# Transposes on TensorE written as float32 products of 32 columns with the identity

## The reference

```python
x = x + _L0_attn_ref(_layernorm(x), Wq, bq, Wk, bk, Wv, bv, Wo, bo, relative_k, relative_v)
x = x + _L0_ffn_ref(_layernorm(x), router_w, router_b, w1, b1, w2, b2, sw1, sb1, sw2, sb2)
...
scores = jnp.einsum('bhld,bhrd->bhlr', Q, K) * scale
scores = scores + jnp.einsum('bhld,lrd->bhlr', Q, rel_k)
attn = jax.nn.softmax(scores, axis=-1)
out = jnp.einsum('bhlr,bhrd->bhld', attn, V)
out = out + jnp.einsum('bhlr,lrd->bhld', attn, rel_v)
```

## Time and profile before

| | us |
|---|---|
| median of 3 runs | 2068.07 (2067.51 to 2069.0) |
| profiled execution, its own time | 2070.57 |
| profiled execution, span of the trace | 2068.8 |
| TensorE busy | 2037.4 |
| DVE busy | 1605.3 |
| ACT busy | 1507.0 |
| GpSimd busy | 1212.4 |

### The profile page before, as it was taken

The page is one execution under the profiler, slowest core; times in us unless marked ns, Lnnn a source line. Parts: engine busy times, 40 slices in busy tenths (PEclk is TensorE's granted clock), DMA queues, the critical chain, the costliest instruction groups (busy, mean ns, idle before and its releaser), DMA issues.

```text
span 2068.8 us, 86886 instructions
## 1 busy us (share of the span) xinstructions
PE 2037.4 (98%) x37378; PEld 1512.6 (73%) x37378; DVE 1605.3 (78%) x3788; ACT 1507.0 (73%) x3333; POOL 1212.4 (59%) x1283
## 2 busy tenths in 40 slices
PE   5999999999999999999999999999999999999999
PEld 3777777777777777777777777777777777777777
DVE  5877897788778877877897788778886767676765
ACT  3767676777677776667667666666666888888887
POOL 4554464456445544554455446444443898989888
PEclk8999999999999999999999999999999999999999
DMA  4212211221221122112211321223122221222120
GB/s 112 74 54 67 76 48 55 76 65 53 56 80 55 49 66 73 56 46 69 76 53 46 84 67 46 57 73 67 46 54 50 27 31 23 33 27 32 24 30 12
DMA packets 256658, 113.05 MB, mean 55 GB/s; under 512 B 143018, under 2 KB 253492, under 8 KB 256276
## 3 DMA queue, kind: packets, MB, share of 16 engines
q1 hardware_dynamic: 255796, 107.10, 21.3%
q10 hardware_dynamic: 480, 0.39, 0.1%
HBM read 83.34 MB, written 8.39 MB: 44 GB/s over the span
## 4 chain that ended last, share of the span: by engine, by line
PE 91%; DVE 4%; ACT 2%; POOL 1%; issue 1%; DMA 1%; SPq 0%; ACTq 0%; DVEq 0%; POOLq 0%
PE ps L1548 21%; PE ps L1483 12%; PE ps L1568 10%; PE ps L1490 8%; PE ps L1578 8%; PE ps L1501 7%; PE ps L1765 3%; PE ps L1767 3%; PE ps L1766 3%; PE ps L1747 3%; PE ps L1749 3%; PE ps L1748 3%; PE ps L1586 1%; ACT probs L777 1%; PE ps L1464 1%; DVE keys L1235 1%
## 5 line engine op out<-in xcount | busy, mean ns | idle before, releaser
L777 ACT ACTIVATE probs<-ps,neg_max 128x512 f32<-128x512 f32 x1024 | 690.4, 686 | 338.7 <-DVE neg_max L1003 338.6
L1003 DVE TENSOR_REDUCE neg_max<-ps 128x1 f32<-128x512 f32 x1024 | 635.8, 683 | 148.9 <-PE ps L1490 144.8
L549 POOL TENSOR_TENSOR stat_hi<-q_twice,mask8h 128x1024 f16<-128x1024 f16 x128 | 242.6, 1895 | 533.4 <-PE ps L1490 481.7
L1548 PE MATMUL ps<-const,probs 128*128 128x128 f32 x4096 | 497.3, 274 | 1.3 <-ACT probs L777 0.5
L1548 PEld LDWEIGHTS ps<-const,probs 128*128 128x128 f32 x4096 | 454.0, 141 | 29.5 <-issue 15.8
L1008 DVE COPY probs_t<-ps 128x512 f32<-128x512 f32 x512 | 339.9, 684 | 89.8 <-PE ps L1548 87.3
L767 ACT ACTIVATE probs_t<-ps 128x512 f32<-128x512 f32 x512 | 278.8, 595 | 131.8 <-PE ps L1548 129.5
L679 POOL TENSOR_TENSOR probs_t<-probs,probs_t 128x1024 f16<-128x1024 f32 x160 | 341.3, 2156 | 31.1 <-ACT probs_t L859 30.4
L1483 PE MATMUL ps<-keys,stat_hi 128*32 128x512 f16 x4096 | 317.4, 383 | 0.0
L1490 PE MATMUL ps<-rk_split,stat_rel 96*32 96x512 f16 (+2 forms) x4096 | 281.4, 340 | 0.0
L565 POOL TENSOR_TENSOR stat_rel<-q_rel,mask4h 96x1024 f16<-96x1024 f16 x128 | 250.6, 1958 | 49.7 <-PE ps L1490 30.6
(11 more groups left out here) (173 smaller groups left out, 2864.6 us busy)
## 6 DMA issues: line engine op xcount, KB each, us to landing
rv_step<-in_rv_win SPq DMA_DIRECT2D x128, 512.0 KB, 3.9
keys<-keys SPq DMA_DIRECT2D x56, 96.0 KB, 2.7
x_pair<-in_x SPq DMA_DIRECT2D x8, 512.0 KB, 4.4
rel_scratch<-rel_t SPq DMA_DIRECT2D x256, 16.0 KB, 3.2
x_pair<-in_x SPq DMA_DIRECT2D x16, 256.0 KB, 3.1
x_pair<-rel_scratch SPq DMA_DIRECT2D x64, 64.0 KB, 4.3
out<-keys SPq DMA_DIRECT2D x16, 256.0 KB, 2.3
q_twice<-q_hi SPq DMA_DIRECT2D x28, 128.0 KB, 3.0
```

The lines of the kernel that those rows point to most:

```text
L777: nc.scalar.activation(probs[:, q, :], ps[:, i, :], ACT.Exp, bias=neg_max[:, q:q + 1], accum_out=row_sum[parity][:, s * QUADS + q:s * QUAD ...
L1003: nc.vector.tensor_reduce(neg_max[:, q:q + 1], ps[:, i, :], op=ALU.max, axis=AX_X, negate=True).then_inc(max_done, 1)
L1548: last = nc.tensor.transpose(ps[:, bank, rt * P:(rt + 1) * P], probs[:, q, rt * P:(rt + 1) * P], ident)
```

## The change

Four places no longer use the transposing form: the probabilities (transposes), the relative sums (rel_transposes), the rows (rows_t) and the natural queries (natural_queries). A new helper, transposed, takes the data in slices of 32 columns as the stationary operand and multiplies each with the identity in a plain float32 matmul; each lands in its 32 partitions of the same PSUM bank. The tile rel_o loses its unused half, and its memset on GpSimd is gone with it. The FFN part's own transposes (relative_sums, prepare_h, prepare_comb) and the float16 ones of relative_queries stay.

```diff
-        rel_o = sb("rel_o", [P, 4, 32])
+        rel_o = sb("rel_o", [P, 2, 32])
...
-        SETUP_POOL = 11
+        SETUP_POOL = 10
...
-            nc.gpsimd.memset(rel_o[:], 0.0).then_inc(setup_pool, 1)
...
+            def transposed(out, rows):
+                for g in range(rows.shape[1] // 32):
+                    last = nc.tensor.matmul(out[32 * g:32 * g + 32, :], rows[:, 32 * g:32 * g + 32], ident, start=True, stop=True, skip_group_check=True)
+                return last
...
-                    last = nc.tensor.transpose(ps[:, bank, t * P:(t + 1) * P], x_pair[:, half * 4 + t, :], ident)
+                    last = transposed(ps[:, bank, t * P:(t + 1) * P], x_pair[:, half * 4 + t, :])
...
-                    last = nc.tensor.transpose(ps[:, bank, l * D:(l + 1) * D], rows, ident)
+                    last = transposed(ps[:, bank, l * D:(l + 1) * D], rows)
...
-                        last = nc.tensor.transpose(ps[:, bank, rt * P:(rt + 1) * P], probs[:, q, rt * P:(rt + 1) * P], ident)
+                        last = transposed(ps[:, bank, rt * P:(rt + 1) * P], probs[:, q, rt * P:(rt + 1) * P])
...
-                nc.tensor.transpose(ps[:, AV_BANK, 3 * P:4 * P], rel_o[:].rearrange("p a r -> p (a r)"), ident).then_inc(rel_tr, 1)
+                transposed(ps[0:64, AV_BANK, 3 * P:4 * P], rel_o[:].rearrange("p a r -> p (a r)")).then_inc(rel_tr, 1)
```

More of the change, by code:

```diff
@@ L1031, in reduce_relative @@
                 dve.wait_ge(rel_tr, START + pair * STEPS + s)
-                nc.vector.tensor_reduce(rel_o[:, 0:2, :].rearrange("p a (g h) -> p (a g) h", h=DK), r_masked[:].rearrange("p g l h -> p g h l"),
+                nc.vector.tensor_reduce(rel_o[:].rearrange("p a (g h) -> p (a g) h", h=DK), r_masked[:].rearrange("p g l h -> p g h l"),
                                         op=ALU.add, axis=AX_X).then_inc(rel_reduced, 1)
```

## The result

The changed kernel takes 2527.49 us (median of 4 runs, 2526.15 to 2529.51), the kernel before 2067.9 in the same series. The ratio is 1.222, with a 95% interval of 1.220 to 1.224. The forecast was 2522. The two profiled executions differ by 455.6 us (2526.15 and 2070.57), the medians by 459.6.

The account below looks back on a forecast made before the run. TensorE, busy 98% of the span, was taken as the bound. The terms 448 + 14 + 11 + 2 - 27 + 11 - 5 gave +454 us, a median of 2522; range 2500 to 2538, upper end 2560 with a slightly late supply.

Parts of the forecast that it names:

- The count of matmuls: On TensorE, a plain float32 product is carried out as two matmuls, each with its own weight load, a transpose as one.
- Term 1: Probabilities: 256 calls of 16 squares, each set of four narrow products 0.219 us against 0.109 for a transpose: +448 us.
- term 5: Weight loads of the probabilities' transposes that stood idle 11.5 us for exponentials: waits end inside longer calls, -5 us.
- Term 2: Relative sums at L1586: 128 squares, two narrow products each, 0.22 us for 0.11: +14 us, at the least no added time.
- Term 3: Rows and natural queries made ahead, 14 calls each, 112 squares: +11 us together, and +2 for 16 squares at the start.
- Term 4: Switches of tile shape between narrow products and full width: -27 us for those lost, +11 us for new ones.
- the 178 and 77 places: Rounds that lose a switch into the transposes (178, 0.15 us each) or gain one behind a full-width piece (77, 0.14 each).
- The first rival: An identity product costs no more than a transpose, one matmul, 0.109 us for a set: some 2052 to 2056, chance 0.04.
- The factor of four: Transposing mode is four times faster for float32, so +1423 us less 21 for switches and waits: about 3470, chance 0.02.
- The range: The forecast's own range for the time, 2500 to 2538 us, from the bounds of terms 2, 4, 5 and the set price.
- The second rival: Instructions don't arrive fast enough for TensorE: at 23 ns each a round takes 10.3 us, about 3420 in all; chance 0.08.

Follow-up runs that it names:

- the first experiment: The changed kernel with one plain float32 product of full width for each square in place of four of 32 columns: 2610.3 us, ratio 1.262.

## Why the prediction was right

- **The count of matmuls** (two for a plain float32 product) held: 32768 entries, and at full width, where nothing but the form changed, 8192 for 4096 and the same loss. The prediction's "nothing but the transposing form has one" is true of float32 alone: half-precision products such as L1483 have one entry each (4096 in the trace, 4096 in the program).
- **Term 1, the price of a set** (+448). A call takes 3.49 us, 0.218 for each set. The run with the probabilities back gives 450 for this term, the waits of term 5 and the late rounds below together; 448 - 5 + some 8 would make 451.
- **Term 2, the sums** (+14). The upper bound was the right one: 0.21 in the chain, and 25 of the expected 27 us with their switches.
- **Term 3, rows and natural queries** (+13 with the start). 12.7 by the difference of two runs.
- **Term 4, switches** (-27 + 11). In the changed kernel 0.14 us into narrow tiles stands in the chain, as forecast, and the 0.15 behind L1583 is gone (3.49 and not 3.65). Measured by itself with a tiny matmul a switch was 0.10. No run varied the 178 and 77 places alone, but the two traces can be laid side by side, each round from its first L1501 (L1506) to the next one. The median round got longer by 1.60 us without a piece and 1.70 with sums (forecast 1.60 and 1.71), by 1.88 and 1.98 with a piece of full width (forecast 1.89 and 2.00), and by 1.94 with natural queries (forecast 1.95). The counts of the kinds are those of the prediction. So the switches hold place by place.
- **Term 5, waits** (-5). This row answers to the earlier trace rows:

```profile
L1431 PEld LDWEIGHTS ps<-const,probs 128*32 128x32 f32 x32768 | 908.4, 109 | 9.6 <-ACT probs L776 5.5
```

  Idle weight loads for the exponentials fell from 11.5 to 5.5 us. In the rounds laid side by side some 5 us of waits fell away, but only half of it in calls, as the term has it (2.5 us in 11 rounds). The rest is in rounds with values, whose own loads had waited for the exponentials. The size is right, the place only in part.
- **The first rival** (one matmul for an identity product) is out by the count. **The factor of four** is out by the length of a call: 3.49 to 1.75 is a factor of two. By the page "TensorE: Matmul & The Clock Gate" of the Trainium skill (Terms) transposing mode is four times faster for float32; no run here shows more than two.
- **The range** doesn't follow from its terms: 14, 6.5, 3 and 5 us below 2522 make 2494 and not 2500, and 5, 3 and 5 above make 2535 and not 2538. The measured time lies inside either.
- **The second rival**, a late supply, was the right place to look for the rest. TensorE's waits that end with "issue" in the changed kernel:

```profile
PE ps L1495 <- issue: 1.2, 3, 0.6
PE ps L1573 <- issue: 1.0, 1, 1.0
...
PE ps L1431 <- issue: 0.5, 2, 0.3
...
PE ps L1488 <- issue: 0.3, 1, 0.3
```

  They are 3.0 us together; the time lies 5.5 above the forecast. The rounds show more than the idle time does: 19 are over 0.06 us longer than the others of their kind, 8.7 us together, where the same products at full width have 0.3. The forecast had nothing for this and came close all the same, because other small terms were a few us too high, as in the rounds with sums (1.98 for 2.00); that part is luck. That these rounds are late for want of instructions is argued from the name "issue" and from the comparison with full width, and stays open. At 15 ns for an instruction over a round the supply nearly keeps up.

## What to carry to other kernels

Count the entries of a line in the trace against the matmuls that the program issues, before a form of TensorE instruction is exchanged: the transposing form of float32 is one matmul, a plain product is two, and the mean duration of one entry hides it. A change that saves switches of tile shape is worth 0.10 to 0.20 us for each switch, here less than the second matmul of a single call (1.75 us). Where a change of form looks dear, one run with the same instructions on half-precision data tells whether the number of instructions is to blame, and one with the new form in the old shape what the form alone costs.

## What the hardware showed that I had not expected

- A plain float32 product of full width is slightly slower than four narrow ones over the same square: 3.57 against 3.49 us for 16 squares, 0.223 to 0.219 for each.
- A stationary operand of 64 columns between one of 32 and one of 128 is a tile shape of its own: with it the first experiment paid 0.34 us more in a round with sums.
- The switch from narrow tiles costs 0.15 us into a float32 transpose and 0.20 into a plain float32 product of the same size (3.77 against 3.57 us for a call).
- TensorE can stand idle in small pieces for nothing that the profile shows, which may be a late supply of instructions: 3.0 us in 2524 with 530 packets in the instruction queue, and 10.4 us on two lines of the half-precision kernel with narrow products, which has fewer instructions but shorter matmuls.
